# A norm-scan-FFN kernel with its first stage rewritten: y = x2 - mean by one multiplication, pair statistics, weights in quarters, eleven x buffers, six scan banks

## The reference

```
def _L0_xattn_ref(q, k, v):          # called with q = LN(x), k = v = ctx
    kv = jnp.swapaxes(k * v, 0, 1)
    def step(r, kv_t):
        r = DECAY * r + kv_t         # DECAY = 0.9, along the 512 rows
        return (r, r)
    ...
    return q * jnp.swapaxes(rs, 0, 1)
def _L0_ffn_ref(x, w1, b1, w2, b2):
    h = jax.nn.relu(quant_linear(x, w1, b1))
    return quant_linear(h, w2, b2)
x = x + _L0_xattn_ref(_layernorm(x, axis=-1), ctx_1024, ctx_1024)
x = x + _L0_ffn_ref(_layernorm(x, axis=-1), L0_ffn_w1, L0_ffn_b1, L0_ffn_w2, L0_ffn_b2)
```

## Time and profile before

| | |
|---|---|
| median of 3 runs | 1306.49 us (1303.84 to 1306.87) |
| profiled execution, its own time | 1307.37 us |
| its span, first to last instruction | 1305.6 us |
| mean granted TensorE clock | 0.979 |
| busy: PE, DVE, ACT, POOL | 1229.4, 909.8, 992.6, 291.0 us |
| DMA | 460.23 MB, 353 GB/s over the span |

### The profile page before, as it was taken

One profiled execution on the slowest core, in us unless ns is written; L12 is line 12 of the kernel. 1 busy time (PEld: TensorE's weight loads), 2 busy tenths in 40 slices (PEclk: granted clock), 3 DMA queues, 4 the chain that ended last, 5 costly groups with the idle time before them and its releaser, 6 DMA issues. The chain is left out here.

```text
span 1305.6 us, 17104 instructions
## 1 busy us (share of the span) xinstructions
PE 1229.4 (94%) x5386; PEld 564.2 (43%) x5386; DVE 909.8 (70%) x1314; ACT 992.6 (76%) x1403; POOL 291.0 (22%) x777
## 2 busy tenths in 40 slices
PE   6768999999599999999999999799999999999998
PEld 2333443434344444444444444344444444444443
DVE  5979999999667777777777777555545545444446
ACT  5688787877767777777777776688888777778794
POOL 2859999999600000000000000000000000000000
PEclk9888999999899999999999999899999999999999
DMA  9887999997489999999999997699999999999997
GB/s 356 330 320 262 343 335 349 328 350 287 184 298 358 368 350 347 363 362 361 349 354 363 363 356 297 246 341 414 415 415 415 415 415 416 415 416 416 416 352 260
DMA packets 136127, 460.23 MB, mean 353 GB/s; under 512 B 10852, under 2 KB 10872, under 8 KB 123512
## 3 DMA queue, kind: packets, MB, share of 16 engines
q1 hardware_dynamic: 82680, 276.86, 54.0%
q10 hardware_dynamic: 53376, 182.47, 39.3%
HBM read 266.35 MB, written 192.94 MB: 352 GB/s over the span
## 5 line engine op out<-in xcount | busy, mean ns | idle before, releaser
L881 PE MATMUL ps<-w2T,xq 128*128 128x512 f16 x2048 | 450.2, 381 | 11.9 <-ACT xq L593 11.4
L839 PE MATMUL ps<-xq,w1T 128*128 128x512 f16 x2048 | 449.8, 381 | 1.4 <-DVE xq L717 1.4
L593 ACT ACTIVATE xq<-xq,hb,hs 128x512 f16<-128x512 f32 x494 | 358.5, 802 | 83.2 <-PE ps L881 61.6
L708 DVE TENSOR_REDUCE work<-xq 128x2 f32<-128x1024 f32 x255 | 311.0, 1220 | 127.0 <-ACT xq L546 127.0
L546 ACT ACTIVATE xq<-ps 128x1024 f32<-128x1024 f32 x255 | 260.9, 1023 | 123.8 <-PE ps L839 123.5
L818 PE MATMUL ps<-xq,work 128*128 128x512 f32 x640 | 291.3, 613 | 30.0 <-ACT xq L481 19.6
L881 PEld LDWEIGHTS ps<-w2T,xq 128*128 128x128 f16 x2048 | 199.3, 98 | 262.8 <-ACT xq L593 26.0
L839 PEld LDWEIGHTS ps<-xq,w1T 128*128 128x128 f16 x2048 | 199.5, 98 | 237.7 <-issue 3.3
L818 PEld LDWEIGHTS ps<-xq,work 128*128 128x128 f32 x640 | 122.8, 195 | 196.1 <-issue 146.1
L756 DVE TENSOR_TENSOR work<-ps,cs_bc 128x512 f32<-128x512 f32 x128 | 87.1, 689 | 98.0 <-PE ps L881 90.8
L481 ACT ACTIVATE xq<-ps,rstd 128x512 f32<-128x512 f32 x128 | 77.9, 688 | 62.1 <-POOL rstd L448 56.3
(11 more groups left out here) (105 smaller groups left out, 577.4 us busy)
## 6 DMA issues: line engine op xcount, KB each, us to landing
hidden_scratch<-xq SPq DMA_DIRECT2D x240, 512.0 KB, 6.1
xq<-hidden_scratch ACTq DMA_DIRECT2D x220, 512.0 KB, 19.8
xq<-in_x_dram SPq DMA_DIRECT2D x32, 1024.0 KB, 7.8
x_scratch<-xq SPq DMA_DIRECT2D x32, 1024.0 KB, 5.7
xq<-in_ctx_dram ACTq DMA_DIRECT2D x31, 1024.0 KB, 5.6
work<-x_scratch ACTq DMA_DIRECT2D x29, 1024.0 KB, 7.9
work<-x_scratch SPq DMA_DIRECT2D x25, 1024.0 KB, 8.3
out_dram<-work SPq DMA_DIRECT2D x24, 1024.0 KB, 15.0
```

Source lines behind the costliest of these rows:

```text
L593: act.activation(hq[c % HQ], src[:, c % 2, :], ACT.Relu, bias=hb[:, q:q + 1], scale=hs[:, q:q + 1]).then_inc(h_scaled, 1)
L708: dve.tensor_reduce(hmax[:, b * NF + 2 * q:b * NF + 2 * q + 2], src, AX.X, ALU.max).then_inc(kept_maxed, 1)
L839: last = pe.matmul(bank, w1T[:, k, f * P:(f + 1) * P], xq_rows(b, k), start=(k == 0), stop=(k == KD - 1))
L881: last = pe.matmul(acc_bank(s, i), src[:, i * P:(i + 1) * P], w2T[:, q, :], start=first, stop=final)
```

## The change

The first stage is written anew; the others change where they meet it.

- **One multiplication.** x2 - mean = (x - mean)(1 + scan / std) = y. ACT forms x - mean in place and 1 + scan / std out of PSUM (`factors`), DVE multiplies the two and takes the row maximum in the same operation (`product`). y is kept and stored instead of x2. The layer norm of y is that of x2; the mean is added back with the bias in the third stage, where `add_bias` becomes a scalar_tensor_tensor.
- **Statistics.** DVE takes all four tiles of x, three batches ahead, and no longer ACT. POOL computes two batches at once in eight columns (`x_stats`, `y_stats`; the first two and the last two batches singly), in rings of four batches.
- **Weights in quarters** of 1 MB, one at every second batch: DVE and POOL at batch 2m + 2, ACT's integers at 2m + 3, PE at 2m + 4, ACT's copy at 2m + 5, through two staging buffers. All eight are turned inside the loop, in PSUM banks 6 and 7; the biases at batch 21.
- **Buffers.** Eleven for x, of which three are those of the later stages, loaded five batches ahead; three for the context; six PSUM banks in a ring for the scan.
- **Order.** The last eleven batches stay in SBUF and are quantized first, so that the second stage loads 21 batches instead of 32. Six of them are stored only during the second stage.
- `turn_x` goes tile by tile and waits for each quantized tile, not for all four. All loops are straight code.

```diff
-XS = 4
-ACT_TILES = 2
-AHEAD = 2
-
+XS = 11
+CS = 3
+RING = 4
+LATE = 6
+LEAD = 5
+BIAS_AT = 21
...
+    parked = list(range(NB - XS, NB))
+    order_b = [b for n in range(XS - NX, XS) for b in parked if b % XS == n]
+    order_b += [b for b in parked if b not in order_b]
+    order_b += list(range(NB - XS))
+    late = list(range(NB - LATE, NB))
...
+    x_groups = [[0], [1]] + [[j, j + 1] for j in range(2, NB, 2)]
+    y_groups = [[j, j + 1] for j in range(0, NB - 2, 2)] + [[NB - 2], [NB - 1]]
...
+    def weights_at(j):
+        m = j // 2 - 1
+        return [m] if j % 2 == 0 and 0 <= m < len(quarters) else []
...
+            sp.dma_start(ct[0], ctx_rows[0]).then_inc(ctx_loaded[0], 16)
+            for j in range(LEAD):
+                load_x(j)
+                if j == 2:
+                    load_weights(0)
...
+            for j in range(NB):
+                if j + LEAD < NB:
+                    load_x(j + LEAD)
+                for m in weights_at(j + 2):
+                    if m > 0:
+                        load_weights(m)
+                if j > 0 and j - 1 not in late:
+                    store_x2(j - 1)
...
+            x_stats(x_group[0])
+            x_stats(x_group[1])
+            for j in range(NB):
+                if j % 2 == 1 and j + 1 < NB:
+                    x_stats(x_group[j + 1])
+                if j % 2 == 0 and j >= 2:
+                    y_stats(y_group[j - 1])
+                for m in weights_at(j):
+                    round_weights(m)
...
+            def factors(j, i):
+                u = j * NI + i
+                if i == 0:
+                    act.wait_ge(stats1_ready, x_group[j] + 1)
+                xi = xt[j % XS][:, i, :]
+                act.activation(xi, xi, ACT.Identity, bias=nmean1[:, u:u + 1])
+                act.wait_ge(scan_ready, u + 1)
+                wait_count(act, x2_done, u + 1 - 2 * NI)
+                act.activation(g1[j % 2][:, i, :], scan_bank(j, i), ACT.Identity, bias=ones[:, 0:1],
+                               scale=rstd1[:, u:u + 1]).then_inc(scan_scaled, 1)
...
+            load_ctx(1)
+            load_ctx(2)
+            square(0)
+            for j in range(NB):
+                factors(j, 0)
+                factors(j, 1)
+                if j + 1 < NB:
+                    square(j + 1)
+                factors(j, 2)
+                factors(j, 3)
+                if j + CS < NB:
+                    load_ctx(j + CS)
+                for m in weights_at(j - 1):
+                    int_weights(m)
+                for m in weights_at(j - 3):
+                    keep_weights(m)
...
+            def product(j, i):
+                if i == 0 and j >= RING:
+                    dve.wait_ge(stats2_ready, y_group[j - RING] + 1)
+                dve.wait_ge(scan_scaled, j * NI + i + 1)
+                xi = xt[j % XS][:, i, :]
+                dve.tensor_tensor_reduce(xi, g1[j % 2][:, i, :], xi, 1.0, -3.0e38, ALU.mult, ALU.max,
+                                         rowmax[:, j % RING * NI + i:j % RING * NI + i + 1]).then_inc(x2_done, 1)
...
+            for j in range(3):
+                for i in range(NI):
+                    x_stats(j, i)
+            for j in range(NB):
+                product(j, 0)
+                x_stats(j + 3, 0)
+                for i in range(1, NI):
+                    product(j, i)
+                    y_stats(j, i - 1)
+                    x_stats(j + 3, i)
+                y_stats(j, NI - 1)
+                for m in weights_at(j):
+                    weight_scales(m)
...
-                dve.tensor_tensor(x2c[out_slot(s)][:, i, :], x2c[out_slot(s)][:, i, :], bq2_bc[:, :], ALU.add).then_inc(bias_added, 1)
+                u = order_b[turns_c[s]] * NI + i
+                dve.scalar_tensor_tensor(x2c[out_slot(s)][:, i, :], x2c[out_slot(s)][:, i, :], nmean1[:, u:u + 1], bq2_bc[:, :],
+                                         ALU.subtract, ALU.add).then_inc(bias_added, 1)
...
+            def scan(j, i):
+                u = j * NI + i
+                wait_count(pe, scan_scaled, u - 5)
...
+            for j in range(NB):
                 pe.wait_ge(ctx_squared, j + 1)
...
+                    scan(j, i)
+                for m in weights_at(j - 2):
+                    turn_weights(m)
...
-                pe.wait_ge(x_scaled, (b + 1) * NI)
                 wait_count(pe, xq_kept, b)
-                for k in range(KD):
-                    for i in range(NI):
+                for i in range(NI):
+                    pe.wait_ge(x_scaled, b * NI + i + 1)
+                    for k in range(KD):
```

More of the change, by code:

```diff
@@ L217, in build @@
         q_scales = sem("q_scales")
-        x2_loaded = [sem(f"x2_loaded{n}") for n in range(3)]
+        x2_loaded = [sem(f"x2_loaded{n}") for n in range(NX)]
         x_scaled = sem("x_scaled")
@@ L334, in _ @@
-            store_x2(NB - 1, XS - 1)
-            sp.wait_ge(w_int, 8)
-            for t in range(3):
-                load_x2(t)
+            for j in range(NB):
[6 more added lines that the diff above has]
+                    store_x2(j - 1)
             for n, b in enumerate(stored):
+                if order_b[b] in late:
+                    store_x2(order_b[b])
@@ L432, in round_weights, with x_stats @@
-            def round_weights(w, k):
-                gp.wait_ge(w_scale, 2 * w + k // 2 + 1)
-                rows = (NF, KD)[w] // 4
-                quarter = w_stage[w][:, k * 4 * D:(k + 1) * 4 * D]
+            def x_stats(g):
+                js = x_groups[g]
+                wait_count(gp, stats1_ready, g)
+                gp.wait_ge(stats1_in, js[-1] + 1)
+                var = row_stats(pw1, stats_of(st1, js), nmean1[:, columns(js)], neg_half)
+                gp.tensor_tensor(rstd1[:, columns(js)], var, neg_half[:, 0:len(js) * NI], ALU.pow).then_inc(stats1_ready, 1)
@@ new lines, in y_stats, with round_weights @@
+            def y_stats(g):
+                js = y_groups[g]
+                wait_count(gp, stats2_ready, g)
+                gp.wait_ge(stats2_in, js[-1] + 1)
+                var = row_stats(pw2, stats_of(st2, js), mean2[:, columns(js)], half)
+                gp.tensor_tensor(zrow[:, columns(js)], stats_of(rowmax, js), mean2[:, columns(js)], ALU.subtract)
+                gp.tensor_tensor(rstd2[:, columns(js)], var, neg_half[:, 0:len(js) * NI], ALU.pow).then_inc(stats2_ready, 1)
+            def round_weights(m):
+                w, k = quarters[m]
+                gp.wait_ge(w_scale, m + 1)
+                rows = (4, 1)[w]
@@ new lines, in scan @@
+            def scan(j, i):
+                u = j * NI + i
+                wait_count(pe, scan_scaled, u - 5)
+                kv, bank = ct[j % CS], scan_bank(j, i)
+                terms = [(k, kv[:, i - k, :]) for k in range(i + 1)]
+                for k, rows in terms:
+                    last = pe.matmul(bank, decay_mat[:, k * P:(k + 1) * P], rows, start=(k == 0), stop=(k == terms[-1][0]))
+                last.then_inc(scan_ready, 1)
+            pe.wait_ge(dve_step, 1)
+            for j in range(NB):
@@ L821, in phase_a @@
-                if isinstance(j, int):
-                    for w, k in weight_quarters(j - 2):
-                        if w == 0:
-                            turn_weights(w, k)
-            batches(pe, phase_a)
-            for k in range(4):
-                turn_weights(1, k)
+                    scan(j, i)
+                for m in weights_at(j - 2):
+                    turn_weights(m)
+                if j == BIAS_AT:
+                    turn_biases()
             def spread(turn):
```

412 lines of the change are left out of this document (151 added, 261 removed).

## The result

| | before | after |
|---|---|---|
| median | 1306.21 us (4 runs) | 1276.46 us (4 runs, 1275.42 to 1277.15) |
| span of the profiled execution | 1305.6 us | 1274.8 us |
| busy PE, DVE, ACT, POOL | 1229.4, 909.8, 992.6, 291.0 | 1216.2, 871.2, 980.4, 162.3 us |
| instructions | 17104 | 15533 |

The ratio is 0.9775 (95% interval 0.9763 to 0.9787): 2.25% faster, 29.8 us. The forecast was 42 us. The time lies in the stated range (1254 to 1282), but outside the forecast's own 1259 to 1271 and inside rival C's 1272 to 1290.

A forecast was written before the change was run, and what follows sets the result against it. POOL's full queue was taken to set the first stage's 9.27 us per batch. First stage -33.1, hand-over -6.7 and PE's turn -1.4 gave -41.2, rounded to -42: 1264.5 us, range 1254 to 1282.

The forecast's parts named there:

- rival C: First-stage loop longer: POOL stretched, products held behind POOL's long instructions, or DMA late; 1272 to 1290 us, chance 0.27.
- The steady batches: First stage behind the weights: PE at its floor, 0.429 us per pass, 20 passes 8.58 us per batch.
- rival C's sign: First stage: PE waiting for ACT's square in every pair would show the forecast wrong; no size given.
- The loop's size: First stage with weights, per two batches: 19.5 us with w1, 18.4 with w2; rounds cost 4.0 and 1.0 us.
- The start: First stage: DVE waits for x3 until about 25 us, statistics follow the first rounding, PE stalls 3.4 us, kept to the end.
- Sum of the first stage: Last scan ends at 294.9 + 3.4 + 5.0 = 303.3 us, 33.1 us earlier than before.
- Hand-over: From last scan to first quantization: 9.3 us instead of 16.0, saves 6.7.
- The turn: Start of the second stage: PE's transposes begin with the first quantized tile, saves 1.4 us.
- Second and third stage: No gain from fewer x2 loads; both stages as long as before, the second 474 us.
- Late stores: Six stores moved into the second stage: cost nothing; uncovered, 1.5 us.
- the bias form: Third stage: dearer bias addition on half idle DVE costs nothing; if it lay open, 13 us.
- Rival B: First stage: the loop never binds, since rounding overlaps or the pair chain is short; -50, 1257 us, chance 0.17.

The follow-up runs named there:

- e5: Changed kernel with POOL's x statistics ahead of the weight rounding and ACT's int conversion, PE's turn and ACT's copy of weights one batch later: 1261.16 us, ratio 0.9657.
- e1: Changed kernel with POOL making the pair's x statistics before it rounds the quarter of weights: 1271.72 us, ratio 0.9733.
- e3: Changed kernel with the first quarter of w1 and the biases loaded behind x3 and x4 instead of before them: 1276.1 us, ratio 0.977.
- e2: Changed kernel with ACT squaring the next context ahead of its batch instead of in its middle: 1272.03 us, ratio 0.9735.
- e6: e5 with the edits of e2 and e3 added, the fastest version: 1257.64 us, ratio 0.963.
- e7: Changed kernel with PE's transposes of x waiting for all four quantized tiles, as before: 1277.71 us, ratio 0.979.
- e11: Changed kernel with one late store instead of six, batches 26 to 30 stored in the first stage: 1276.87 us, ratio 0.9776.
- e12: Changed kernel with the plain bias addition of before, mean not added back, so the output is not the reference's: 1276.83 us, ratio 0.9774.
- e10: Changed kernel with x loaded three batches ahead instead of five: 1275.61 us, ratio 0.9764.
- e4: Changed kernel with the edits of e1, e2 and e3 together: 1269.7 us, ratio 0.972.

## Why the prediction was right, and where its sum was short

- **Sign, place, mechanism: right in the main.** The steady batches run at PE's floor (8.61 us for the 8.58 forecast), PE waits only between 21 and 203 us, and the weight phase runs in a loop through POOL's rounding and its pair statistics. The sum of that loop's links (20.94) shows it, and e5, which cuts both branches behind the rounding, brings PE's own period. Two signs came out otherwise: PE idles in nine pieces instead of three or four, and it waits for ACT's square in every pair with weights, which I had named as rival C's sign.
- **The loop's size: the term that failed.** Forecast 19.5 and 18.4 us, measured 20.94 and 19.57: 3 x 1.44 + 4 x 1.17 = 9.0 us, and excess over PE's own period 14 instead of 5. ACT's first tile and DVE's batch took 9.98, not 8.5, in every round: a tile costs ACT 1.5 and its square stands in mid-batch, so that DVE waits 1.14 us. With w1 the rounding took 4.1, not 3.5. POOL's chain was right (4.0 to 4.4 for 4.3); its power went from 1.01 us at four columns to 1.64 at eight, between the two bounds.
- **A branch that I did not list.** ACT's conversion and copies follow the rounding as POOL's statistics do, 0.2 to 0.6 us shorter. The branch costs nothing in the changed kernel, but because of it e1 alone gave 4.7 instead of 13.7 us.
- **Rival C** has the time (1272 to 1290), and of its causes two in part: the rounding stretched by 0.6 us with w1, and a product held behind a long rounding (1.85 us at 133.81 in the changed kernel), outside the loop. The larger part of the miss, 1.5 us in each of seven rounds, is none of its causes. So the time lies in C's range mostly for a reason that C does not name.
- **The start: nearly the right size, half of its cause wrong.** I expected DVE to be held by x3 and PE to wait 3.4 us at batch 5. DVE did wait for x3 until 25.25, but e3, which removes this, changes nothing. PE waited 2.60 us at 21.3, since ACT's square of context 1 stands behind two tiles that wait for POOL until 19.36, and was slow again after it; e2 and e6, which move the square, have no such wait. The other half was right: 1/std of batches 4 and 5 behind the first rounding came at 57.14 (forecast 55.6), and e1, which moves it ahead, starts batch 5 at 59.73 instead of 61.69 (forecast 60).
- **Sum of the first stage.** 1.7 (start) + 9.0 (loop) + 0.8 (13 last batches at 8.64) = 11.5 of the 11.7 us between 303.3 and 315.05. The second stage, 1.2 us shorter than forecast, hides a part of it. The recorded -42 is no rounding of -41.2; the sum itself gives 1265.3 us.
- **Hand-over: right.** 315.05 to 324.24 is 9.2 us (forecast 9.3), saves 6.8 of 16.0. The turn saves 1.28 (forecast 1.4), shown by e7.
- **Second and third stage: right.** Late stores (e11) and the bias form (e12) cost nothing. The second stage is 1.2 us shorter: PE's first 16 passes took 4.96 us instead of 6.12. So the 11 loads that fall away gave nothing that can be seen.
- **DMA: right that it does not bind, for a needless reason.** I let eleven buffers absorb a deficit at 379 GB/s. The changed kernel moved 409 GB/s over 61.69 to 82.63 (364 over the whole 61.69 to 202.79, where the loop sets the pace), e5 406 over 69.55 to 196.36, and three batches ahead did as well (e10). The Trainium skill's figure of about 358 GB/s (DMA: Bandwidth & Descriptors, Where 436 GB/s comes from) is passed here too. The 4 us that I estimated from it do not follow from my numbers: 10.3 less 9.1 us over 16 batches would be 19 us, less what the early loads take up.
- **Rival B (1257) was the right picture of the floor**, and wrong about this kernel: it took e6 to get there, 1257.64.

## What to carry to other kernels

When weights or other extra work ride along in the queues of a steady loop, write the ring (the loop of waits) down: who starts after whom, once around, with every instruction that stands between in each in-order queue, until the sum is the period. Busy shares said nothing here (PE 87, ACT 85, DVE 82, POOL 56% over 61.69 to 82.63); a ring of 20.94 us did, and two edits of order, without less work, gave 15 us (e5). Where two branches leave the same instruction, cutting the longer one gains only what the other is shorter. A wait inside a supposed ring is no link of it: it points to the engine through which the real ring goes, as ACT's 1.02 us for the rounding did in e1.

In these queues it paid to put first what is ready earliest: statistics before rounding, and a conversion one batch after its input.

## What the runs showed of the hardware

- A DVE operation on two SBUF tiles was held by one long POOL instruction. In e1's timeline:

```profile
168.66 1.98 POOL L445 TENSOR_SCALAR xq<-xq,isw 128x2048 f32<-128x2048 f32 x1
...
169.28 1.89 DVE L630 CUSTOM_DVE_ANT_0 xq<-xq 128x512 f32<-128x512 f32 x1
```

The multiplication took 1.89 instead of 0.68 us and ended 0.5 us after POOL. The Trainium skill (SBUF — State Buffer, SBUF: two separate sides) says that of the two whichever starts first holds the shared port for its whole instruction; this pair of rows agrees. It costs DVE about 1.2 us in a batch where DVE had room.

- PE's slow passes. In the changed kernel the 40 passes behind waits of 0.62 to 1.25 us took 17.43 us. Behind 2.62 us they took 19.13 at 82.63 and 17.43 at 124.51. In e1 they took 19.13 behind both waits of 2.29 us, and the granted clock was 0.92 over 80.35 to 100.96, between the two levels of 1.2 and 2.4 GHz. In e4 the 40 passes at 96.96 took 20.40 us behind a wait of only 0.62, but PE had idled another 2.04 us just before, ahead of the transposes. Inside the loop this cost nothing: pairs with slow and with fast passes took the same 20.94 us (20.6 in e1). Where PE sets the pace it does: at the start 80 passes took 36.30 us behind 2.60, and 34.60 in e1 behind 1.78.
- POOL's power took 1.01 us at four columns and 1.64 at eight: 0.16 us per further column between these two.
